# A routed expert kernel: earlier gathers for the first group of a two-group pass, a second group routed in the prologue, own row buffers for each pass

## The chip, the cores and the metric

The kernel runs on one core of a Trainium2 chip. The metric is the device time of one execution in microseconds. A core has five engines with instruction streams of their own: PE (matrix products), DVE (vector work), ACT (activations, copies out of PSUM), POOL (here: indirect transfers) and SP (here: plain transfers). Each runs its stream in order and waits on semaphores.

## What is computed

`x` has 8 units (batch entries) of 512 tokens by 128 channels. Three sublayers follow one another: half a mixture-of-experts layer, a recurrent token mixer, and half the same mixture-of-experts layer again, each on normalised input and added to `x`.

```python
def ffn(x, gate_w, w1, w3, w2):                 # 8 experts, 2 for each token
    probs = softmax(x @ gate_w)
    weights, experts = top_k(probs, 2);  weights /= weights.sum(-1)
    for i in range(8):
        h = silu(x @ w1[i]) * (x @ w3[i])       # 128 -> 512
        out += (h @ w2[i]) * weight_of_expert_i
x = x + 0.5 * ffn(layernorm(x))
x = x + mixer(layernorm(x))                     # k, v, r projections, a scan over 512 tokens, output projection
x = x + 0.5 * ffn(layernorm(x))
```

## The kernel before

**Runs and passes.** The work of the two expert layers is cut into 9 runs (lines 38 to 63). Runs 0 to 3 are the first layer, two units each. Runs 4 to 8 are the second layer, with 2, 2, 2, 1 and 1 units. A pass is a list of rows in memory sorted by expert, each expert's rows padded to tiles of 128. In the first layer each run is a pass of its own; in the second, runs 4 and 5 share a pass, runs 6 and 7 share one, and run 8 has its own. In a shared pass the first run (`OPEN`) computes only its full tiles, and the second (`MORE`) fills up and computes the partly filled ones. There are 177 tiles (steps). Runs begin at tiles 0, 23, 46, 69, 92, 101, 131, 140 and 162; `PEND`, the end of the pass, is 23, 46, 69, 92, 131, 131, 162, 162, 177.

**A tile.** SP loads sorted rows from `rows_in` into `rin`, six loads ahead (line 663; a load holds one or two tiles). PE turns them (line 1228), ACT copies them to `rT` (line 770). PE makes the two up products `pa` and `pb` (line 1237), ACT applies SiLU (line 799), DVE multiplies to `h` (line 1115), PE makes the down product three tiles later (line 1251), ACT copies it and stores it to `rows_out` (lines 780, 786). PE's tile `t` waits for `h` of tile `t-2`.

**Routing.** For each run: norm, split in two 16-bit parts `hi` and `lo`, transposed product with the gate (`turn`, `xnT`, `logits`, `keep`), then choosing (`CHOOSE`, line 90: `pick` to `place2`, `scatter`, `tiles`, `weights`; DVE functions at lines 938 to 1079). POOL then writes the tokens' rows to their slots in `rows_in`: 8 indirect transfers for each unit (`scatter`, line 717). When the tiles of a pass are stored, POOL reads each token's two result rows back: 8 indirect transfers for each unit (`gather`, line 730), and DVE adds them to `x` (`combine`, line 1117). Three gather buffers rotate (`GSLOTS`). After a first-layer combine follows the mixer of that unit, and then the routing of the second-layer run that needs it.

**Zero fills.** Rows that no token takes must be defined, so SP fills `rows_in` from a zero row (lines 614 to 660). There are four memory sets, used by passes 0 to 3 and again by 4 to 6. Sets 0 and 1 are filled, 23 tiles each, by one transfer ahead of the tiles (`FILLED_FIRST`); sets 2 and 3 and the longer tails of sets 0 and 1 in pieces of 256 rows, one per tile from tile 0 (list `later`). A run's first scatter waits until the fills of its set have landed (lines 720 to 725).

**The order.** A planner in the file (`make_plan`, line 218) decides behind which tile each step stands on every engine. It has costs for each step (`WORK`), a model clock for each engine, due times, a few corrections by hand (`DUE_SHIFT`, and `NOT_BEFORE`, earliest tiles for named steps), and it books POOL's transfers by due time, one for each 1.6 us of its own clock (`SPACE`). Steps in `soon(...)` (lines 252 to 265) stand ahead of tile 0 in the order written: the prologue. There run 0 is routed, and run 1 is normalised and its logits kept; run 1's choosing stands among tiles 0 to 9. On POOL a memset (line 755) spaces the transfers.

```python
def send(tile, until):          # line 337: books transfers up to the model time `until`
    ...
        due, asked, name, run, many = first = min(now)          # 344
        free["pool"] = max(free["pool"], asked) + SPACE         # 345
        transfers.append((tile, name, run, *many.pop(0)))       # 346
```

In the order before, run 1's scatters stand at tiles 10 to 18, run 2's at 24 to 27 (nine) and 39 to 41 (seven), run 0's gathers at 28 to 38, run 6's scatters at 120 to 127, run 7's at 134 and 135, run 4's gathers at 136 to 145, run 5's up to 160 with run 8's scatters between, those of runs 6 and 7 from 167. The combines of run 0 stand at tiles 35 and 39, those of run 5 at 163.

Of the kernel before, what the change touches and what calls it, by code (L numbers as in the profile page):

```python
# [21 lines left out]
F32 = mybir.dt.float32  # L22
F16 = mybir.dt.float16
# [4 lines left out]
P = 128  # L28
B, S, D = 8, 512, 128
E, F, TOPK = 8, 512, 2  # L30
FC = F // P
JU = S // P
T = 128
# [4 lines left out]
FIRST = ((2,), (2,), (2,), (2,))  # L38
SECOND = ((2, 2), (2, 1), (1,))
PASSES = FIRST + SECOND  # L40
UNITS = tuple(n for units in PASSES for n in units)
R1 = sum(len(units) for units in FIRST)
RUNS = len(UNITS)
PASS = tuple(i for i, units in enumerate(PASSES) for _ in units)
OPEN = tuple(r + 1 < RUNS and PASS[r + 1] == PASS[r] for r in range(RUNS))
MORE = tuple(r > 0 and OPEN[r - 1] for r in range(RUNS))
SET = tuple(i if i < len(FIRST) else i - len(FIRST) for i in PASS)
SETS = max(SET) + 1
U0 = tuple(sum(UNITS[0 if r < R1 else R1:r]) for r in range(RUNS))
UG = max(UNITS)  # L50
JG = UG * JU
# [5 lines left out]
NQ = tuple(SINGLES + PAIRS[r] if PAIRS[r] else (STEPS[r] + 1) // 2 for r in range(RUNS))  # L57
START = tuple(sum(STEPS[:r]) for r in range(RUNS + 1))
PSTART = tuple(sum(PASS_STEPS[:PASS[r]]) for r in range(RUNS))
PEND = tuple(sum(PASS_STEPS[:PASS[r] + 1]) for r in range(RUNS))  # L60
QSTART = tuple(sum(NQ[:r]) for r in range(RUNS + 1))
ROWS = tuple(max(PASS_STEPS[PASS[r]] for r in range(RUNS) if SET[r] == g) * T for g in range(SETS))
TILES = START[RUNS]
assert all(len(units) <= 2 for units in PASSES) and sum(UNITS[:R1]) == sum(UNITS[R1:]) == B
assert all(OPEN[r] or MORE[r] or STEPS[r] == 2 * PAIRS[r] + SINGLES for r in range(RUNS))
# [12 lines left out]
GSLOTS = 3  # L78
RING = 6
SKEW = 3  # L80
FILLED_FIRST = 2
FILL = 256
PACE = 544
PACES = 4
# [133 lines left out]
def make_plan():  # L218
# [9 lines left out]
    def route(run, normed):  # L228

        chain(CHOOSE, run, 0, (START[run], 0), 0.0, normed)  # L230

    never = 1e9
    route(1, [])
    for run in range(2, R1):
        route(run, [chain(NORM, run, b, (START[run], 1), 0.0) for b in range(UNITS[run])])
    for g in range(R1):
# [6 lines left out]
                route(run, [chain(NORM, run, b, (START[run], 1), 0.0, [mixed[U0[run] + b]])  # L243
                            for b in range(UNITS[run])])
    for run in range(R1, RUNS):
        for b in range(UNITS[run] if PEND[run] < TILES else 0):
            gathered[run, b] = chain(FINISH, run, b, (START[min(run + 2, RUNS - 1)], 3), never)


# [2 lines left out]
    def soon(run, *steps):  # L252
        plan.extend((EARLY, step, run, b) for step, b in steps)
# [6 lines left out]
        soon(0, *[("split", 2)][:b + 1 not in first], ("keep", b))  # L260
        soon(0, *((step, b + 1) for step in ("xnT",) if b + 1 in first))
    soon(0, *((step, 0) for step in CHOOSE))
    soon(1, *(("stats", b) for b in one), ("rsqrt", 0))
    soon(0, *(("split", e) for e in range(3, E)))
    soon(1, *((step, b) for b in one for step in ("norm", "turn", "xnT", "hi", "lo", "logits", "keep")))

    clock, transfers, waiting = Clock(), [], []
    free, held, freed = clock.free, {}, {}
# [58 lines left out]
    def ask(at, due, name, run, units):  # L327

        waiting.append([due, at, name, run, [(b, j, c) for b in units for j in range(JU) for c in range(TOPK)]])

    def in_use(run, unit):

        order = [p[2:] for p in plan if p[1] == "gather"]
        n = order.index((run, unit))
        return n >= GSLOTS and "combine" not in gathered[order[n - GSLOTS]].ends
# [39 lines left out]
    for tile in range(TILES):  # L375
        clock.tile(tile)
        for run in range(RUNS):
            if tile == PEND[run] + SKEW:
                for b in range(UNITS[run]):
                    ask(free["pe"] + LAND, tile + (8 if run < R1 else 60) + 4 * MORE[run] + b, "gather", run, [b])  # L380
                    plan.append((tile, "gather", run, b))
        send(tile, free["pe"])
        begun = free["pe"]
        limits = {"dve": begun + SLIP["dve"], "act": begun + SLIP["act"], "pe": begun + SLIP["pe"]}
        found = choose(limits)
        while found:
            put(found[0], tile, found[1])
            found = choose(limits)
        while any(tile >= START[run] - LEAD and left[run] for run in left) or (
                tile == TILES - 1 and any(c.next() for c in chains)):  # L390
            found, sent = choose(None), len(transfers)
            if found:
                put(found[0], tile, found[1])
            send(tile, 1e8)
            assert found or len(transfers) > sent
    last = [(TILES, step, run, b) for run in range(RUNS) if PEND[run] == TILES
            for step in ("gather", "combine", "write") for b in range(UNITS[run])]
    return plan + last, transfers, clock

# [41 lines left out]
def macaron_kernel(nc, x, channel_vecs, att_w, gate, w1, w3, w2, out):  # L441
    with ExitStack() as ctx:
# [6 lines left out]
        def sem(name):  # L449
            return ctx.enter_context(nc.semaphore(name))  # L450


        rows_in = [nc.dram_tensor(f"rows_in{g}", (ROWS[g], 2 * D), F16, kind="Internal").ap() for g in range(SETS)]
        rows_out = [nc.dram_tensor(f"rows_out{g}", (ROWS[g], D), F32, kind="Internal").ap() for g in range(SETS)]


        xres = sb("xres", [P, B * JU, D])
# [89 lines left out]
        s_stage = [sem(f"stage_in{i}") for i in range(E)]  # L547
        s_w2 = sem("w2_in")
        s_zrow = sem("zrow_made")
        s_fill = [sem(f"rows_zeroed{g}") for g in range(SETS)]  # L550
        s_rest = [sem(f"more_rows_zeroed{g}") for g in range(SETS)]
        s_const = sem("const_made")
        s_uphi = sem("up_hi_made")
        s_uplo = sem("up_lo_made")
# [59 lines left out]
        def pieces(g, start, end, size):  # L614

            return [(g, at, min(at + size, end)) for at in range(start, end, size)]

        fills = [pieces(g, 0, PASS_STEPS[g] * T, ROWS[g] if g < FILLED_FIRST else FILL) for g in range(SETS)]
        rests = [pieces(g, PASS_STEPS[g] * T, ROWS[g], FILL) for g in range(SETS)]


        @block.sync
        def _(sp):
# [7 lines left out]
            def fill(piece, filled):  # L631

                g, start, end = piece
                rows = rows_in[g][start:end, :].rearrange("(r p) c -> p r c", p=P)
                sp.dma_start(rows, zrow[:, None, :].to_broadcast([P, (end - start) // P, 2 * D])).then_inc(filled[g], 16)
# [19 lines left out]
                             w2[e, :, :].rearrange("(c p) d -> p c d", p=P)).then_inc(s_w2, 16)  # L655
            for g in range(2, R1):
                load_x(g)
            for piece in fills[1]:
                fill(piece, s_fill)
            later = [(piece, s_fill) for g in range(2, SETS) for piece in fills[g]]  # L660
            later += [(piece, s_rest) for g in range(SETS) for piece in rests[g]]

            def load(q):
                t = FIRST_STEP[q]
                run, n = run_of(t), TILE_OF[t][2]
                if t == START[run]:
                    sp.wait_ge(s_scat[run], 16 * TOPK * JU * UNITS[run])
                wait(sp, s_turn, q - SLOTS + 1)
                at = (t - PSTART[run]) * T
                sp.dma_start(rin[:, q % SLOTS, 0:n, :],  # L670
                             rows_in[SET[run]][at:at + n * T, :].rearrange("(n p) c -> p n c", p=P)
                             ).then_inc(s_rin[q % SLOTS], 16)

            def step(name, run, b):
# [27 lines left out]
        def _(pool):  # L702
# [12 lines left out]


            def scatter(run, b, j, c):
                g = SET[run]
                at = (U0[run] + b) * JU + j
                if (b, j, c) == (0, 0, 0):  # L720
                    pool.wait_ge(s_slots, run + 1)
                    pool.wait_ge(s_lo, max(count(("lo", "lo_m"), ("lo", run, i)) for i in range(UNITS[run])))
                    pool.wait_ge(s_fill[g], 16 * len(fills[g]))
                    if run >= R1 and rests[g]:
                        pool.wait_ge(s_rest[g], 16 * len(rests[g]))
                pool.indirect_dma_start(  # L726
                    rows_in[g][:], bass.IndirectOffsetOnAxis(ap=slot[:, c, at:at + 1], axis=0),
                    parts[:, at, :], None).then_inc(s_scat[run], 16)

            def gather(run, b, j, c):  # L730
                at = (U0[run] + b) * JU + j
                if (b, j, c) == (0, 0, 0):
                    for k in range(YSLOTS):
                        pool.wait_ge(s_yst[k], 16 * len(range(k, PEND[run], YSLOTS)))
                n = GATHERS.index((run, b))
                if (j, c) == (0, 0) and n >= GSLOTS:
                    pool.wait_ge(s_comb, count(("combine",), ("combine", *GATHERS[n - GSLOTS])))
                pool.indirect_dma_start(  # L738
                    yg[:, n % GSLOTS, c, j, :], None, rows_out[SET[run]][0:PASS_STEPS[PASS[run]] * T, :],
                    bass.IndirectOffsetOnAxis(ap=slot[:, c, at:at + 1], axis=0)).then_inc(  # L740
                        s_last[j] if n + 1 == len(GATHERS) else s_gat[n % GSLOTS], 16)

            def every(run, units):
                return [(run, b, j, c) for b in units for j in range(JU) for c in range(TOPK)]
# [9 lines left out]
                    wait(pool, s_pace, sent - PACES + 1)  # L754
                    pool.memset(pace[:, sent % PACES, :], 0).then_inc(s_pace, 1)  # L755
            for run in range(RUNS):
                for one in every(run, range(UNITS[run] if PEND[run] == TILES else 0)):
                    gather(*one)


# [1 line left out]
        def _(act):  # L762
# [23 lines left out]
            def store(t):  # L786
                run = run_of(t)
                at = (t - PSTART[run]) * T
                act.wait_ge(s_yrow, t + 1)
                act.dma_start(rows_out[SET[run]][at:at + T, :], yrow[:, t % YSLOTS, :]  # L790
                             ).then_inc(s_yst[t % YSLOTS], 16)

            def tile(t):
# [602 lines left out]
```

## Time and profile before

| | |
|---|---|
| median of 3 runs | 611.98 us (611.75 to 612.49) |
| the profiled execution | 611.98 us |
| its span, first to last instruction | 610.1 us |
| PE matrix products | 517.9 us busy, 85% |
| DVE | 423.6 us, 69% |
| ACT | 318.7 us, 52% |
| POOL | 389.0 us, 64% |
| DMA traffic | 59.55 MB, mean 98 GB/s |
| granted TensorE clock, mean | 0.980 |

Busy times overlap, since the engines run side by side. The first 54 us are the prologue, with PE mostly idle; the last 24 us hold the end of PE's work and the last gathers. "Busy" of PE is modelled from pipelined matmuls and is not its peak. A granted clock of 1.00 is 2.4 GHz, 0.50 is 1.2 GHz.

### The profile page before, as it was taken

The numbers are of one execution on the slowest core, as the hardware profiler recorded it, in microseconds if no ns is written. First come the engines' busy times: TensorE is split into PE (matmuls) and PEld (weight loads), VectorE is DVE, ScalarE is ACT, GpSimd is POOL, SyncE is SP. The second block draws the span as 40 slices with busy tenths as digits, with TensorE's granted clock in tenths as the row PEclk, the third lists the DMA queues.
The fourth block names the chain that finished last, engine by engine and source line by source line (L and its number), as shares of the span: only waits on it lengthen the run. The fifth ranks groups of instructions, "written<-read, shape, count | busy, mean of one in ns | idle before, by whom it ended". The sixth has DMA issues, their size and how long they took to land.

```text
span 610.1 us, 18551 instructions
## 1 busy us (share of the span) xinstructions
PE 517.9 (85%) x5866; PEld 474.2 (78%) x5866; DVE 423.6 (69%) x1218; ACT 318.7 (52%) x703; POOL 389.0 (64%) x490
## 2 busy tenths in 40 slices
PE   1234899999999899998999989999999999999930
PEld 1233789898988789877898779898788899998930
DVE  4861963556878998889999895887788766225431
ACT  5432664444584666666585654676465454444410
POOL 1171049499999990399935999102957998955973
PEclk9999999999999999999999999999999999999985
DMA  8963233555232222212321133111121442323332
GB/s 280 328 209 110 69 92 110 145 148 127 83 105 79 67 80 57 71 62 70 83 71 46 58 113 92 45 51 32 53 84 54 122 111 88 102 62 105 85 91 60
DMA packets 89062, 59.55 MB, mean 98 GB/s; under 512 B 10256, under 2 KB 82704, under 8 KB 88976
## 3 DMA queue, kind: packets, MB, share of 16 engines
q1 hardware_dynamic: 55296, 29.97, 16.9%
q0 software_dynamic: 8192, 16.79, 9.0%
q10 hardware_dynamic: 25488, 11.61, 6.7%
q8 instruction: 58, 0.95, 0.7%
q14 instruction: 28, 0.23, 0.1%
HBM read 28.65 MB, written 29.69 MB: 96 GB/s over the span
## 4 chain that ended last, share of the span: by engine, by line
PE 55%; DVE 14%; ACT 12%; POOL 8%; issue 7%; DMA 3%; POOLq 0%; ACTq 0%; DVEq 0%; SPq 0%
PE py L1260 17%; PE pa L1246 14%; PE pb L1246 12%; POOL rows_in L726 3%; ACT xn L818 3%; DVE h L1115 3%; POOL yg L738 3%; PE bkB L1319 2%; PE pT L1233 2%; PE bkB L1298 2%; ACT sil L799 2%; POOL pace L755 2%; PE bkA L1313 2%; DVE stats L905 2%; PE bkA L1298 1%
## 5 line engine op out<-in xcount | busy, mean ns | idle before, releaser
L726 POOL DMA_INDIRECT rows_in<-parts,slot x128 | 134.9, 1054 | 175.7 <-DVE slot L1040 153.8
L1260 PE MATMUL py<-ffn_w,h 128*128 x1416 | 196.2, 282 | 9.4 <-ACT yrow L784 9.0
L1115 DVE TENSOR_TENSOR h<-sil,pb 128x512 f32<-128x512 f32 x177 | 120.7, 686 | 116.8 <-ACT sil L799 76.6
L1260 PEld LDWEIGHTS py<-ffn_w,h 128*128 128x128 f32 x1416 | 172.6, 192 | 15.5 <-issue 12.3
L1246 PE MATMUL pa<-rT,ffn_w 128*128 128x128 f16 (+1 forms) x1752 | 150.3, 232 | 14.9 <-DVE h L1115 11.8
L1246 PE MATMUL pb<-rT,ffn_w 128*128 128x128 f16 (+1 forms) x1752 | 154.4, 232 | 0.0
L738 POOL DMA_INDIRECT yg<-rows_out,slot x128 | 125.1, 978 | 35.0 <-issue 22.8
L1246 PEld LDWEIGHTS pa<-rT,ffn_w 128*128 x1752 | 123.3, 99 | 29.5 <-issue 18.4
L755 POOL MEMSET pace<- 128x544 uint8 x223 | 127.6, 572 | 0.2
L1246 PEld LDWEIGHTS pb<-rT,ffn_w 128*128 x1752 | 121.8, 98 | 6.9
L799 ACT ACTIVATE sil<-pa 128x512 f32<-128x512 f32 x177 | 105.4, 595 | 31.8 <-PE pa L1246 31.7
L784 ACT ACTIVATE yrow<-py 128x128 f32<-128x128 f32 x177 | 48.4, 274 | 85.3 <-PE py L1260 81.1
L779 ACT ACTIVATE rT<-pT 128x512 f16<-128x512 f16 (+1 forms) x112 | 56.8, 507 | 67.6 <-PE pT L1233 63.0
L1233 PE MATMUL pT<-ident,rin 128*128 128x128 f16 x354 | 38.6, 221 | 9.6 <-DMA rin<-rows_in 9.6
L818 ACT ACTIVATE xn<-xres,shift,rstd 128x128 f32<-128x128 f32 x96 | 39.3, 486 | 8.3 <-DVE shift L927 7.0
L1125 DVE SCALAR_TENSOR_TENSOR xres<-yg,wts,xres 128x128 f32<-128x128 f32 x120 | 34.1, 347 | 9.0 <-DMA yg<-rows_out,slot 8.5
L1313 PE MATMUL bkA<-ident,xn 128*128 128x128 f32 x64 | 11.8, 315 | 28.0 <-ACT xn L818 27.2
L1233 PEld LDWEIGHTS pT<-ident,rin 128*128 128x128 f16 x354 | 25.8, 99 | 10.9 <-DMA rin<-rows_in 9.8
L1313 PEld LDWEIGHTS bkA<-ident,xn 128*128 128x128 f32 x64 | 8.5, 165 | 29.3 <-issue 28.1
L935 DVE TENSOR_TENSOR parts<-xn,parts 128x512 f16<-128x512 f32 x24 | 16.4, 688 | 10.5 <-ACT parts L832 10.5
L1298 PE MATMUL bkB<-xT,qkv_w 128*128 128x512 f16 x96 | 23.4, 380 | 0.3 <-ACT xT L848 0.3
L905 DVE BATCH_NORM_STATS2 stats<-xres 128x6 f32<-128x128 f32 x96 | 20.9, 280 | 4.0 <-DMA xres<-in_x 3.5
(156 smaller groups left out, 458.8 us busy)
## 6 DMA issues: line engine op xcount, KB each, us to landing
rows_out<-yrow ACTq DMA_DIRECT2D x177, 64.0 KB, 1.9
rin<-rows_in SPq DMA_DIRECT2D x65, 128.0 KB
rows_in<-zrow SPq DMA_DIRECT2D x34, 128.0 KB, 2.1
shared<-in_w SPq DMA_DIRECT2D x16, 256.0 KB, 6.7
rin<-rows_in SPq DMA_DIRECT2D x47, 64.0 KB
rows_in<-zrow SPq DMA_DIRECT2D x2, 1472.0 KB, 11.2
xres<-in_x SPq DMA_DIRECT2D x4, 512.0 KB, 6.5
ffn_w<-in_w SPq DMA_DIRECT2D x8, 256.0 KB, 4.7
```

The source lines that it names most:

```text
L726: pool.indirect_dma_start(rows_in[g][:], bass.IndirectOffsetOnAxis(ap=slot[:, c, at:at + 1], axis=0), parts[:, at, :], None).then_inc(s_sc ...
L738: pool.indirect_dma_start(yg[:, n % GSLOTS, c, j, :], None, rows_out[SET[run]][0:PASS_STEPS[PASS[run]] * T, :], bass.IndirectOffsetOnAxis( ...
L755: pool.memset(pace[:, sent % PACES, :], 0).then_inc(s_pace, 1)
L779: act.activation(rT[:, q % 2, :, 0:n], pT[:, :, 0:n], ACT.Copy).then_inc(s_rT, 1)
L784: act.activation(yrow[:, t % YSLOTS, :], py[:], ACT.Copy).then_inc(s_yrow, 1)
L799: act.activation(sil[:, t % 2, :], pa[t % 2][:], ACT.Silu, scale=1.0 / WS).then_inc(s_sil, 1)
L818: ins = act.activation(xn[:, at, j, :], xres[:, js, :][:, j, :], ACT.Identity, bias=shift[:, u, j:j + 1], scale=rstd[:, u, j:j + 1])
L1115: dve.tensor_tensor(h[:, t % RING, :], sil[:, t % 2, :], pb[t % 2][:], ALU.mult).then_inc(s_h, 1)
L1233: mm = pe.transpose(pT[:, part, n * T:(n + 1) * T], rin[:, q % SLOTS, n, part * D:(part + 1) * D], ident16[:])
L1246: mm = pe.matmul(bank[:, i * cols:(i + 1) * cols], weight_bytes[:, bass.ds(experts[expert_of(t)] * 4 + at, 2 * P)].bitcast(F16), rT[:, q % ...
L1260: mm = pe.matmul(py[:], h[:, step % RING, at:at + T], w, start=(c == 0), stop=(c == FC - 1))
L1298: mm = pe.matmul(bank[:], qkv_w[:, f, wp, :], xT[:, u % 2, xp, start:start + S], start=(n == 0), stop=(n == 5))
```

## The change

- A gather waits for the end of its own run's rows, `GEND`, in place of the end of the pass, `PEND`. The rows of an opening run all lie in the first 23 tiles of its pass (`HEAD_STEPS`). `GEND` is 23, 46, 69, 92, 115, 131, 154, 162, 177, so it differs for runs 4 (115 for 131) and 6 (154 for 162). The planner asks for gathers three tiles after it.
- Run 1's choosing stands in the prologue, behind the splits 3 to 7, and its scatters are asked for at time 0. In the prologue both its norms now stand ahead of those splits, and its two `lo` steps behind its other steps.
- Each pass has its own `rows_in` and `rows_out`. All of them are filled; the one transfer ahead of the tiles is pass 0's, the others are pieces of 256 rows, one per tile from tile 0: pass 1 at tiles 0 to 11, pass 2 at 12 to 23, pass 3 at 24 to 35, then passes 4 to 6 up to tile 79. A first scatter waits for the pieces of the head of its pass.

`DUE_SHIFT` and `NOT_BEFORE` stay as they are.

```diff
-SET = tuple(i if i < len(FIRST) else i - len(FIRST) for i in PASS)
-SETS = max(SET) + 1
...
-PEND = tuple(sum(PASS_STEPS[:PASS[r] + 1]) for r in range(RUNS))
+HEAD_STEPS = tuple((units[0] * S * TOPK + E * (T - 1)) // T for units in PASSES)
+
+GEND = tuple(PSTART[r] + (HEAD_STEPS if OPEN[r] else PASS_STEPS)[PASS[r]] for r in range(RUNS))
...
-FILLED_FIRST = 2
...
-    route(1, [])
...
-    soon(1, *(("stats", b) for b in one), ("rsqrt", 0))
+    soon(1, *(("stats", b) for b in one), ("rsqrt", 0), *(("norm", b) for b in one))
     soon(0, *(("split", e) for e in range(3, E)))
-    soon(1, *((step, b) for b in one for step in ("norm", "turn", "xnT", "hi", "lo", "logits", "keep")))
+    soon(1, *((step, b) for b in one for step in ("turn", "xnT", "logits", "hi", "keep")), *(("lo", b) for b in one))
+    soon(1, *((step, 0) for step in CHOOSE))
...
+    ask(0.0, START[1] - 3, "scatter", 1, range(UNITS[1]))
...
-            if tile == PEND[run] + SKEW:
+            if tile == GEND[run] + SKEW:
...
-        fills = [pieces(g, 0, PASS_STEPS[g] * T, ROWS[g] if g < FILLED_FIRST else FILL) for g in range(SETS)]
-        rests = [pieces(g, PASS_STEPS[g] * T, ROWS[g], FILL) for g in range(SETS)]
+        fills = [pieces(g, 0, HEAD_STEPS[g] * T, FILL if g else HEAD_STEPS[g] * T) for g in range(len(PASSES))]
+        rests = [pieces(g, HEAD_STEPS[g] * T, PASS_STEPS[g] * T, FILL if g else PASS_STEPS[g] * T)
+                 for g in range(len(PASSES))]
...
-            for piece in fills[1]:
-                fill(piece, s_fill)
-            later = [(piece, s_fill) for g in range(2, SETS) for piece in fills[g]]
-            later += [(piece, s_rest) for g in range(SETS) for piece in rests[g]]
+            for piece in rests[0]:
+                fill(piece, s_rest)
+            later = [(piece, filled) for g in range(1, len(PASSES)) for many, filled in ((fills, s_fill), (rests, s_rest))
+                     for piece in many[g]]
...
                     pool.wait_ge(s_fill[g], 16 * len(fills[g]))
-                    if run >= R1 and rests[g]:
+                    if MORE[run]:
                         pool.wait_ge(s_rest[g], 16 * len(rests[g]))
...
-                        pool.wait_ge(s_yst[k], 16 * len(range(k, PEND[run], YSLOTS)))
+                        pool.wait_ge(s_yst[k], 16 * len(range(k, GEND[run], YSLOTS)))
...
-                    yg[:, n % GSLOTS, c, j, :], None, rows_out[SET[run]][0:PASS_STEPS[PASS[run]] * T, :],
+                    yg[:, n % GSLOTS, c, j, :], None, rows_out[PASS[run]][0:(GEND[run] - PSTART[run]) * T, :],
```

## Rows read from the trace of the kernel before

**Rows 1.** Busy times from 57 to 587 us, sum of six stretches (length, then each engine).
```profile
sum 530.00, PE 502.79 PEld 461.51 DVE 388.62 ACT 294.73 POOL 359.28; mean PE 83.80 PEld 76.92 DVE 64.77 ACT 49.12 POOL 59.88
```
**Rows 2.** DMA issues by line: KB each, median us from issue to landing.
```profile
rows_in<-zrow SPq DMA_DIRECT2D x34, 128.0 KB, 2.1
...
yg<-rows_out,slot POOLq DMA_INDIRECT x128, 2.7
```
**Rows 3.** Timeline of ACT, prologue: start us, us, engine, line, operation, [idle before].
```profile
22.45 4.83 ACT L768 ACTIVATE ffn_w<-shared 128x1024 f16<-128x1024 f32 x5
32.83 1.65 ACT L818 ACTIVATE xn<-xres,shift,rstd 128x128 f32<-128x128 f32 x4 [5.55 <-DVE shift L927]
...
44.00 0.20 ACT L840 ACTIVATE logit<-bkB 128x32 f32<-128x32 f32 x1 [1.51 <-PE bkB L1319]
...
54.12 0.84 ACT L772 ACTIVATE qkv_w<-yg 128x768 f16<-128x768 f32 x1
...
56.27 0.60 ACT L799 ACTIVATE sil<-pa 128x512 f32<-128x512 f32 x1
```
**Rows 4.** Timeline of DVE, prologue.
```profile
19.17 0.22 DVE L950 TENSOR_REDUCE mx<-logit 128x8 f32<-128x64 f32 x1
...
27.80 0.16 DVE L1079 TENSOR_SCALAR wts<-ed 128x8 f32<-128x8 f32 x1
...
43.20 0.16 DVE L1091 TENSOR_SCALAR omix<-vecs 128x3 f32<-128x3 f32 x1
...
44.60 0.27 DVE L1096 TENSOR_SCALAR yg<-att_raw,omix 128x128 f32<-128x128 f32 x1
```
**Rows 5.** Timeline of PE, tiles 2 and 5.
```profile
60.07 0.89 PE L1246 MATMUL pa<-rT,ffn_w 128*128 128x256 f16 x6
...
68.04 0.81 PE L1246 MATMUL pa<-rT,ffn_w 128*128 128x256 f16 x6 [1.80 <-DVE h L1115]
```
**Rows 6.** Timeline of SP's queue, tiles 11, 17, 23 (and 24).
```profile
86.54 0.33 SPq L635 DMA_DIRECT2D rows_in<-zrow  x1
...
112.71 0.36 SPq L670 DMA_DIRECT2D rin<-rows_in  x1
...
121.59 2.31 SPq L635 DMA_DIRECT2D rows_in<-zrow  x2
```
**Rows 7.** Timeline of POOL: first and last (16th) scatter of run 1, first of run 2.
```profile
83.35 1.15 POOL L726 DMA_INDIRECT rows_in<-parts,slot  x1 [33.86 <-DVE slot L1040]
...
109.38 0.96 POOL L726 DMA_INDIRECT rows_in<-parts,slot  x1 [0.16 <-issue]
...
118.66 0.96 POOL L726 DMA_INDIRECT rows_in<-parts,slot  x1 [7.75 <-DVE slot L1040]
```
**Rows 8.** Timeline of PE, tile 22: run 1's first rows are turned.
```profile
118.51 0.39 PE L1233 MATMUL pT<-ident,rin 128*128 128x128 f16 x4
```
**Rows 9.** Timeline of DVE: the two combines of run 0.
```profile
152.82 2.31 DVE L1125 SCALAR_TENSOR_TENSOR xres<-yg,wts,xres 128x128 f32<-128x128 f32 x8
...
163.35 2.31 DVE L1125 SCALAR_TENSOR_TENSOR xres<-yg,wts,xres 128x128 f32<-128x128 f32 x8
```
**Rows 10.** Timeline of POOL: last scatter of run 6, first of run 7.
```profile
450.54 0.97 POOL L726 DMA_INDIRECT rows_in<-parts,slot  x1 [0.16 <-issue]
...
459.65 0.96 POOL L726 DMA_INDIRECT rows_in<-parts,slot  x1 [7.41 <-DVE slot L1040]
```
**Rows 11.** Timeline of SP's queue: run 7's first two loads.
```profile
475.06 0.90 SPq L670 DMA_DIRECT2D rin<-rows_in  x2
```
**Rows 12.** Timeline of PE, tile 139: run 7's first rows are turned.
```profile
482.62 0.39 PE L1233 MATMUL pT<-ident,rin 128*128 128x128 f16 x4
```
**Rows 13.** Stretch of 10 us: busy times, granted clock, DMA share, GB/s.
```profile
360.00:370.00 10.00, 7.95 (x85) 7.57 (x83) 7.83 (x12) 3.82 (x8) 9.18 (x12) 0.83 0.39 111
```
**Rows 14.** Timeline of POOL: first of the last eight gathers.
```profile
591.00 0.94 POOL L738 DMA_INDIRECT yg<-rows_out,slot  x1 [0.30 <-issue]
```
**Rows 15.** Timeline of ACT's queue: the last store.
```profile
586.88 0.33 ACTq L790 DMA_DIRECT2D rows_out<-yrow  x1
```

More of the change, by code:

```diff
@@ L59 @@
 PSTART = tuple(sum(PASS_STEPS[:PASS[r]]) for r in range(RUNS))
-PEND = tuple(sum(PASS_STEPS[:PASS[r] + 1]) for r in range(RUNS))
+HEAD_STEPS = tuple((units[0] * S * TOPK + E * (T - 1)) // T for units in PASSES)
+GEND = tuple(PSTART[r] + (HEAD_STEPS if OPEN[r] else PASS_STEPS)[PASS[r]] for r in range(RUNS))
 QSTART = tuple(sum(NQ[:r]) for r in range(RUNS + 1))
-ROWS = tuple(max(PASS_STEPS[PASS[r]] for r in range(RUNS) if SET[r] == g) * T for g in range(SETS))
 TILES = START[RUNS]
@@ L245, in make_plan @@
     for run in range(R1, RUNS):
-        for b in range(UNITS[run] if PEND[run] < TILES else 0):
+        for b in range(UNITS[run] if GEND[run] < TILES else 0):
             gathered[run, b] = chain(FINISH, run, b, (START[min(run + 2, RUNS - 1)], 3), never)
@@ L395, in make_plan @@
             assert found or len(transfers) > sent
-    last = [(TILES, step, run, b) for run in range(RUNS) if PEND[run] == TILES
+    last = [(TILES, step, run, b) for run in range(RUNS) if GEND[run] == TILES
             for step in ("gather", "combine", "write") for b in range(UNITS[run])]
@@ L450, in sem @@
             return ctx.enter_context(nc.semaphore(name))
-        rows_in = [nc.dram_tensor(f"rows_in{g}", (ROWS[g], 2 * D), F16, kind="Internal").ap() for g in range(SETS)]
-        rows_out = [nc.dram_tensor(f"rows_out{g}", (ROWS[g], D), F32, kind="Internal").ap() for g in range(SETS)]
+        rows_in = [nc.dram_tensor(f"rows_in{g}", (PASS_STEPS[g] * T, 2 * D), F16, kind="Internal").ap() for g in range(len(PASSES))]
+        rows_out = [nc.dram_tensor(f"rows_out{g}", (PASS_STEPS[g] * T, D), F32, kind="Internal").ap() for g in range(len(PASSES))]
         xres = sb("xres", [P, B * JU, D])
@@ L549, in macaron_kernel @@
         s_zrow = sem("zrow_made")
-        s_fill = [sem(f"rows_zeroed{g}") for g in range(SETS)]
-        s_rest = [sem(f"more_rows_zeroed{g}") for g in range(SETS)]
+        s_fill = [sem(f"rows_zeroed{g}") for g in range(len(PASSES))]
+        s_rest = [sem(f"more_rows_zeroed{g}") for g in range(len(PASSES))]
         s_const = sem("const_made")
@@ L670, in load @@
                 sp.dma_start(rin[:, q % SLOTS, 0:n, :],
-                             rows_in[SET[run]][at:at + n * T, :].rearrange("(n p) c -> p n c", p=P)
+                             rows_in[PASS[run]][at:at + n * T, :].rearrange("(n p) c -> p n c", p=P)
                              ).then_inc(s_rin[q % SLOTS], 16)
@@ L717, in scatter @@
             def scatter(run, b, j, c):
-                g = SET[run]
+                g = PASS[run]
                 at = (U0[run] + b) * JU + j
@@ L756, in _ @@
             for run in range(RUNS):
-                for one in every(run, range(UNITS[run] if PEND[run] == TILES else 0)):
+                for one in every(run, range(UNITS[run] if GEND[run] == TILES else 0)):
                     gather(*one)
@@ L789, in store @@
                 act.wait_ge(s_yrow, t + 1)
-                act.dma_start(rows_out[SET[run]][at:at + T, :], yrow[:, t % YSLOTS, :]
+                act.dma_start(rows_out[PASS[run]][at:at + T, :], yrow[:, t % YSLOTS, :]
                              ).then_inc(s_yst[t % YSLOTS], 16)
```

## The prediction

> **What bounds the kernel now.** I read the busy times of the stretch of tiles first. From tile 0 to the last down product PE works 502.8 of 530 us [rows 1], so it is the bound there and 27 us are all that could be won in the tiles; a wait put in front of PE is lost. Ahead of tile 0 stand 54 us of prologue, behind it a tail. Next I read the five queues one by one. In the tiles POOL sends one transfer per 1.7 us (fifteen steps in 26.0 us [rows 7]: transfer, memset, issue), and it is strictly in order: whatever stands ahead of a transfer delays it. SP is in order as well: its zero fills stand one per tile in the loop, behind a wait for a y copy some three tiles back. In the tail PE has ended, the last store is issued at 586.9 [rows 15], and POOL begins the last unit's eight gathers at 591.0 [rows 14], because it is still busy with those of runs 6 and 7. The end comes 19.1 us behind that start (span 610.1).
>
> **The change part by part.** The profiled execution took 611.98 us, which is also the median of the runs; the sum is made against that.
>
> *1. Run 1 is routed in the prologue.* Routing a group takes DVE from 19.2 to 28.0, 8.7 us [rows 4]. Between the end of `weights` (44.9) and tile 0 DVE has nothing to do, so most of it is covered. But the order ahead of it changes too: both norms of run 1 now precede the splits 3 to 7 on ACT, where before the splits ran first, from 22.5 for 4.8 us, while ACT would otherwise wait for rstd until 32.8 [rows 3]. Now they follow the norms. Run 1's last logits were copied at 44.0; with 4.8 us of splits in the chain that is 48.8, less some 1.2 for the transposes that PE makes meanwhile: 47.6. Then DVE: choosing 8.7, `weights` 1.7 (43.2 to 44.9 [rows 4]): 58.0. ACT's qkv copy waits for that, and from its start to the first SiLU are 2.15 us (54.12 to 56.27 [rows 3]): SiLU at 60.2, product at 60.9. PE starts tile 2 at 61.6 instead of 60.07 [rows 5]. The DVE chain behind it (tile 1's product, the qkv split, tile 2's product, then run 2's statistics, for which PE already waits 1.8 us at 68.04 [rows 5]) is late by the same. **+1.5**, bounds 0 (cover holds) and +3.5.
>
> *2. The same work is gone from tiles 0 to 9:* 8.7 us of DVE. At PE's mean idle share, 27 of 530 us [rows 1], the 63 us from tile 0 to tile 22 hold 3.2 us, and part of that is ACT's. **-1.0**, bounds -3.2 and 0.
>
> *3. Run 1's scatters.* Their slots are ready by 56, yet `scatter` waits for all of `fills[1]`. Those 2944 rows were one transfer ahead of the tiles; now they are 12 pieces issued at tiles 0 to 11. The piece of tile 11 goes out at 86.54 in this trace [rows 6] and a piece lands 2.1 us later [rows 2]: first scatter at 88.7 instead of 83.35 [rows 7], 5.4 late. Nothing else stands behind it on POOL until run 2. But SP's load of run 1's first rows, at 112.7 [rows 6], becomes 118.1 and lands (no row has a load's landing; a piece of equal size takes 2.1) at 120.2, while PE wants them at 118.5 [rows 8], 1.7 of waiting; some of it may fall together with PE's wait for routing run 2. **+1.5**, bounds 0 and +2.5.
>
> The Trainium skill (DMA: Bandwidth & Descriptors, Rules for kernel authors) says to issue a DMA early and wait for its semaphore late. The change does the reverse with this fill; by that rule an early fill would hide and part 3 would cost nothing. The rows show the pace of the tiles in it instead.
>
> *4. Run 2's scatters and run 0's gathers.* SP stands at tile 17 in the load just named, so fills 17 to 23 wait behind it; run 2 needs the one of tile 23. Before, it went out 8.9 us after the load (121.59 [rows 6]); now at 127.0 if the whole distance stays, at 123.1 if SP catches up with PE. Landed: 125.2 to 129.1; I take 127.5. Run 2's first scatter was at 118.66 [rows 7], so POOL is 8.8 late, 7.3 against tiles that are 1.5 late. Behind nine of these scatters stand run 0's sixteen gathers: the eighth starts near 145.7 and lands at 148.4 (2.7 [rows 2]), the sixteenth near 159.3, landing 162.0. Their combines stand at 152.8 and 163.4 on DVE [rows 9]: slacks 4.4 and 1.4. DVE stalls 2.9 and then 3.0 more. At the first PE has next to no slack; at the second it has heavy products of its own ahead. **+4.0**, bounds +2 and +6. Clock after it: **+0.5**.
>
> *5. Gathers of runs 4 and 6 from tile 118 and 157, instead of 134 and 165.* The planner books one POOL transfer per 1.6 us of its own time. Run 6's sixteen scatters stand at tiles 120 to 127 in its order; run 7's are held back by `"scatter7.0": 133`. Before, nothing was asked in between, and on the chip run 7's first scatter went right when its slots came, 459.65 [rows 10]. Now run 4's gathers are asked at 118, and at two per tile some 13 of them are booked between. POOL is free of run 6 at 452.2 [rows 10]; 13 x 1.7 later it is 474.3, so run 7 starts 14.6 late. SP's load of its first rows at 475.06 [rows 11] becomes 489.7, landed 491.8; PE wants them at 482.6 [rows 12], in tile 139. **+9.0**, bounds +4 (10 gathers ahead) and +11. SP waits in that load, but its other loads are for run 7 too. DVE's earlier combine (2.3 us) lies inside the stall.
>
> *6. The clock after that stall.* In the stretch from 360 to 370, with PE busy 7.95 of 10 us, the granted clock was 0.83 [rows 13]: it fell to 1.2 GHz for a while, which is 1.7 us of PE. **+1.5**, bounds 0 and +3. The Trainium skill (TensorE: Matmul & The Clock Gate, Part 1) also has the idle array at 1.2 GHz, and says not to fit a ramp; by it I would put 0 here.
>
> *7. The tail.* With eight gathers of run 6 sent earlier POOL is free when the last store lands, near 586.88 + 2 [rows 15]; start at 588.9 instead of 591.0: **-2.1**. `"combine5.0": 163` stays, so the two combines at tile 163 still block DVE, and run 6's second unit still waits for their slot. A combine more among the last tiles: **+0.5**.
>
> *8. At nothing:* own rows for each pass mean 44 more fills of 128 KB at tiles 36 to 79, one per tile, a stretch in which SP otherwise issues only loads, six tiles ahead of their use, and in which no scatter is ready so early; if that cover fails, each delays a load by up to 2.1 us [rows 2]. Gather ranges are only shorter.
>
> Sum: +1.5 - 1.0 + 1.5 + 4.0 + 0.5 + 9.0 + 1.5 - 2.1 + 0.5 = +15.4: **627 us**.
>
> **Rivals.** *Run 7 is not displaced* (gathers booked behind its scatters): parts 5 and 6 go, +4.9, 617. For: run 6's scatters are late enough in the plan that a small shift decides; against: fifteen tiles lie between ask and hold. 16%. *The fills do not bite* (PE early enough to pull them, DVE free): parts 1 to 4 give 0, +8.9, 621. 14%. *Faster:* neither bites because the prologue absorbs both and only the DVE relief and the tail count: -1.0 - 2.1 + 0.5, 609.4. It decides the matter when run 7's first load goes out by 480.5 (5.4 us of slack) and the first combine finds its rows. 10%. *Nothing moves:* gains and small waits cancel within 1.2 us. 7%.
>
> **Numbers.** The forecast, both waits, 53%, own range 620 to 633. A measurement here tells 0.2%, 1.2 us. Faster 0.10, same 0.07, slower 0.83. Range 613 to 633: it takes in the forecast and the two one-sided cases (83%, less what lies beyond the bounds).
>
> **What would show it.** Right: run 1's first scatter starts just after the fill of tile 11; POOL is idle before run 2's first scatter with a fill as the releaser; DVE waits for yg before the first two combines; gathers stand between run 6's and run 7's scatters; PE waits 7 to 10 us for rin in tile 139 and runs slow behind it; the last gathers start 2 us after the last store. Wrong: no idle PE ahead of tile 139, or the first combine without a wait. If the time is under 613, part 5 has failed.

## The result, and the profile after

The changed kernel takes 628.54 us (median of 4, 627.42 to 630.67) where the kernel before takes 612.00: 1.027 times as long, 95% interval 1.0242 to 1.0304. The profiled execution took 627.73 us with a span of 625.9; the span before was 610.1, so the rows below have to explain 15.8 us.

The page of the changed kernel first: PE's busy time, then its busy share and its granted clock in 40 equal slices of the span:

```profile
PE 521.3 (83%) x5866; PEld 476.8 (76%) x5866; DVE 426.2 (68%) x1218; ACT 319.1 (51%) x703; POOL 394.7 (63%) x499
...
PE   1234899999699899998999989998999599999940
...
PEclk9999999999799999999999999999999899999995
```

The same two lines of slices before:

```profile
PE   1234899999999899998999989999999999999930
...
PEclk9999999999999999999999999999999999999985
```

PE does the same 5866 instructions. Two slices stand out, the 11th (156 to 172 us) and the 32nd (485 to 501 us), each in part idle and at a lower clock. The waits of PE, by what it waited for (us in total, times, longest us), show what it waited for there, after and then before:

```profile
PE pa L1247 <- DVE h L1116: 19.1, 14, 5.7
PE pT L1234 <- DMA rin<-rows_in: 11.0, 4, 7.5
```

```profile
PE pa L1246 <- DVE h L1115: 11.8, 12, 2.0
PE pT L1233 <- DMA rin<-rows_in: 9.6, 2, 9.0
```

The 9.0 us before are a wait ahead of tile 0.

The useful measure is the start of the product (h) of each tile on DVE's timeline, after against before. This table gives the difference in us, worked out from such starts:

```
tile             0    1    12    20    23    30    36    40    44   100   102   131   134   139   146   170   176   span
after - before  3.1  1.0  -0.5  -0.4   0.7  -0.4   5.7   8.0   6.9   7.4   5.9   6.6   8.7  14.2  17.0  17.0  17.9  15.8
```

**The first loss, tile 36.** POOL's timeline, with the last number in brackets the idle time before: run 1's first scatter, run 2's first scatter, run 0's first gather.

```profile
88.44 0.96 POOL L727 DMA_INDIRECT rows_in<-parts,slot  x1 [38.22 <-DMA rows_in<-zrow]
...
128.21 0.96 POOL L727 DMA_INDIRECT rows_in<-parts,slot  x1 [12.66 <-DMA rows_in<-zrow]
...
143.52 0.98 POOL L739 DMA_INDIRECT yg<-rows_out,slot  x1 [0.16 <-issue]
```

Both first scatters now wait for a zero fill; against [rows 7] they are 5.1 and 9.6 us later. SP's queue shows the link between them: it stood in run 1's load from 101 us, with run 2's last fills behind it.

```profile
100.82 0.36 SPq L636 DMA_DIRECT2D rows_in<-zrow  x1
116.29 0.36 SPq L671 DMA_DIRECT2D rin<-rows_in  x1
116.69 0.47 SPq L636 DMA_DIRECT2D rows_in<-zrow  x1
...
124.08 1.73 SPq L636 DMA_DIRECT2D rows_in<-zrow  x2
```

The eighth gather of run 0 completes the rows of its first unit. DVE waits for them, and PE for DVE:

```profile
155.31 0.95 POOL L739 DMA_INDIRECT yg<-rows_out,slot  x1 [0.16 <-issue]
```

```profile
158.46 2.31 DVE L1126 SCALAR_TENSOR_TENSOR xres<-yg,wts,xres 128x128 f32<-128x128 f32 x8 [5.92 <-DMA yg<-rows_out,slot]
...
171.33 2.32 DVE L1126 SCALAR_TENSOR_TENSOR xres<-yg,wts,xres 128x128 f32<-128x128 f32 x8 [1.05 <-DMA yg<-rows_out,slot]
```

```profile
163.06 1.46 PE L1247 MATMUL pa<-rT,ffn_w 128*128 128x128 f16 x12 [5.69 <-DVE h L1116]
```

**The second loss, tile 139.** POOL after run 6's scatters: first and last of 13 gathers of run 4, then run 7's first scatter, 21.7 us later than in [rows 10].

```profile
458.86 0.98 POOL L739 DMA_INDIRECT yg<-rows_out,slot  x1 [0.17 <-issue]
...
479.61 0.95 POOL L739 DMA_INDIRECT yg<-rows_out,slot  x1 [0.16 <-issue]
481.30 1.01 POOL L727 DMA_INDIRECT rows_in<-parts,slot  x1 [0.17 <-issue]
```

PE turns run 7's first rows only after this wait; in [rows 12] there was none:

```profile
498.26 0.61 PE L1234 MATMUL pT<-ident,rin 128*128 128x128 f16 x4 [7.45 <-DMA rin<-rows_in]
```

**The clock behind each.** Stretches of 2 us; the columns are window, length, busy time (instructions) of PE, PEld, DVE, ACT and POOL, granted clock, DMA share, GB/s.

```profile
162.00:164.00 2.00, 0.94 (x10) 0.94 (x11) 1.86 (x7) 0.00 (x0) 1.77 (x3) 0.50 0.25 66
164.00:166.00 2.00, 2.00 (x20) 2.00 (x19) 1.76 (x9) 1.23 (x4) 1.83 (x3) 0.50 0.20 54
166.00:168.00 2.00, 2.00 (x15) 1.94 (x15) 0.78 (x3) 1.93 (x6) 1.84 (x3) 0.56 0.31 85
...
498.00:500.00 2.00, 1.74 (x17) 1.74 (x17) 0.00 (x0) 1.09 (x3) 1.69 (x3) 0.50 0.93 234
500.00:502.00 2.00, 1.97 (x10) 1.67 (x8) 0.69 (x1) 1.97 (x5) 1.83 (x3) 0.50 1.02 304
502.00:504.00 2.00, 1.97 (x25) 1.77 (x25) 0.69 (x1) 0.94 (x3) 1.83 (x3) 0.93 0.35 91
```

After each idle time PE works at 0.50 (1.2 GHz) for 4 to 5 us. As an estimate, busy time times the missing clock gives 0.94 x 0.50 + 2.00 x 0.50 + 2.00 x 0.44 = 2.4 us behind the first and 2.0 us behind the second.

**The two ends.** In the prologue the first product comes at 60.53 and PE starts tile 2 at 61.46 ([rows 5]: 60.07). In the tail POOL has been idle for 11.5 us when its last eight gathers start. The profile names no releaser; in the code they wait for the stores, and the last store was issued at 604.10, 2.6 us ahead (4.1 us before, [rows 14] and [rows 15]):

```profile
604.10 0.33 ACTq L791 DMA_DIRECT2D rows_out<-yrow  x1
```

```profile
606.73 0.95 POOL L739 DMA_INDIRECT yg<-rows_out,slot  x1 [11.52 <-issue]
```

### The profile page after: what moved, and what is told of

It is laid out like the page before. It is cut to its first block, busy times and chain, and to the rows that moved or that the text cites. A ratio compares the mean times of both kernels' runs of the same rounds, so it can differ in the third digit from the quotient of the medians.

```text
span 625.9 us, 18574 instructions
## 1 busy us (share of the span) xinstructions
PE 521.3 (83%) x5866; PEld 476.8 (76%) x5866; DVE 426.2 (68%) x1218; ACT 319.1 (51%) x703; POOL 394.7 (63%) x499
## 4 chain that ended last, share of the span: by engine, by line
PE 38%; POOL 24%; DVE 13%; ACT 11%; issue 7%; DMA 5%; POOLq 0%; ACTq 0%; DVEq 0%; SPq 0%
PE py L1261 12%; PE pa L1247 9%; POOL rows_in L727 9%; POOL pace L756 8%; PE pb L1247 8%; POOL yg L739 6%; ACT xn L819 3%; DVE h L1116 2%; PE bkB L1320 2%; ACT sil L800 2%; PE bkB L1299 2%; PE pT L1234 2%; DVE xres L1126 1%; DMA yg<-rows_out,slot 1%; DVE stats L906 1%
## 5 line engine op out<-in xcount | busy, mean ns | idle before, releaser
L756 POOL MEMSET pace<- 128x544 uint8 x232 | 133.0, 573 | 0.2
L1320 PEld LDWEIGHTS bkB<-gate_w,xnT 128*128 128x128 f32 x128 | 18.8, 226 | 8.3 <-issue 7.2
L1320 PE MATMUL bkB<-gate_w,xnT 128*128 128x8 f32 x128 | 18.9, 275 | 7.3 <-ACT xnT L837 7.3
```

The lines of the kernel that those rows point to most:

```text
L1320: mm = pe.matmul(bkB[:, j * E:(j + 1) * E], xnT[:, j * P:(j + 1) * P], gate_w[:], start=True, stop=True)
```

## The experiments

My theory had two independent causes: the fill of run 1's rows in pieces, and run 4's gathers booked ahead of run 7's scatters. Of the first four runs one undoes the first cause, one the second, one both, and one makes the prologue's change alone. "Before" in each result is the kernel before, timed beside it.

**e1, the fill whole again** (in the changed kernel; `fills` and `later` in `sync`, lines shortened to what changes):

```
-  fills: FILL if g else HEAD_STEPS[g] * T
+  fills: FILL if g > 1 else HEAD_STEPS[g] * T
+  for piece in fills[1]:
+      fill(piece, s_fill)
-  later: for g in range(1, len(PASSES))
+  later: for g in range(2, len(PASSES))
```

> The changed kernel with the fill of run 1's rows as one transfer ahead of the tiles again; all else as in the change. Fill theory (the 12 pieces at tiles 0 to 11 make run 1's scatters late, SP then stands in run 1's load with run 2's fills behind it, POOL is late for run 0's gathers, DVE waits for yg and PE for DVE): the loss of 7 us between tile 35 and tile 44 goes, about 621.5 us; run 1's first scatter near 60, run 2's first scatter near 119, DVE's first two combines without a wait of over 2 us. Rival (the loss comes from the new prologue, which starts the tiles 3 us late and orders DVE's steps otherwise): 628 to 629 us as before the edit, tile 36 still 5 to 6 us late. Second rival (the two losses are one and the same slack: PE late at tile 36 gives POOL time at tile 139, so that without the first the second grows): 626 or more, tile 139 later against tile 138 by over 10 us.

Measured: 623.42 us (621.02 to 627.2) beside 612.03, ratio 1.0149 to 1.0243. The product of tile 40 is 0.2 us late against before, not 8.0. The second loss stays what it was: 1.7 us late at tile 131, 12.2 at tile 146. Both rivals fall. The runs scatter more than I expected, and the median is 2 us over my number. The edit also puts run 2's pieces back to tiles 0 to 11; e9 below takes the two fills apart.

**e2, run 4's gathers late in the plan:**

```
-  if tile == GEND[run] + SKEW:
+  if tile == (sum(PASS_STEPS[:PASS[run] + 1]) if run == 4 else GEND[run]) + SKEW:
```

> The changed kernel, but the planner asks for run 4's gathers only at the tile at which it did before the change (end of the pass); the fills stay in pieces. Theory (13 gathers ahead of run 7's scatters make its rows late): no gather between run 6's and run 7's scatters, PE's wait of 7.45 us at tile 139 and the half clock behind it go, about 618.5 us. Rival (tile 139 is late because run 7's slots are late: run 3's mixing, DVE's order or the combine moved forward): 628 us, the wait at tile 139 stays over 5 us.

Measured: 618.38 us beside 612.03, ratio 1.0085 to 1.0119. POOL's idle time ahead of run 7's scatters is as long as in [rows 10], and its cause is the slots:

```profile
467.54 0.96 POOL L727 DMA_INDIRECT rows_in<-parts,slot  x1 [7.40 <-DVE slot L1041]
```

PE turns run 7's rows without a wait; tile 131 and tile 146 are both 7.9 us late. So nothing of the second loss is left, the 2.1 us that the table has between tiles 131 and 134 among it.

**e3, both edits:**

> Both edits together. Theory: both losses go and are independent, so that only the new prologue, the relief of DVE in tiles 0 to 9 and the earlier gathers of run 6 in the tail are left: 611 us, between 609.5 and 612.5. Rival (the prologue costs 3 us that nothing gives back): 614 to 615. Rival (44 more fills cost PE time): a loss spread over tiles 36 to 79, over 613.

Measured: 611.47 us beside 612.03, ratio 0.9980 to 0.9999. The losses are nearly additive: by the spans (625.9 changed, 621.0, 617.0, 610.8) the fill costs 6.2 us where it stands alone, the gathers 10.2, and together 15.1. From tile 44 to tile 100 the shift stays at 1.8 us. With run 1's fill whole there are 68 small fills where the kernel before has 36 and the change 80, so 32 of the 44 more are in it, at tiles 36 to 67, and they cost nothing.

**e6, run 1 routed in the prologue and nothing else** (on the kernel before):

```
-    route(1, [])
-    soon(1, *(("stats", b) for b in one), ("rsqrt", 0))
+    soon(1, *(("stats", b) for b in one), ("rsqrt", 0), *(("norm", b) for b in one))
...
+    soon(1, *((step, 0) for step in CHOOSE))
...
+    ask(0.0, START[1] - 3, "scatter", 1, range(UNITS[1]))
```

> The kernel before with nothing but run 1 routed in the prologue (fill of run 1 whole, memory shared, gathers as before). Theory: tile 0 is 3 us late, the tiles give 2 to 3 us back by tile 20, run 1's scatters start near 60: 612 us, between 611 and 613. Rival (the prologue makes the loss at tile 36): 617 us or more. Rival (first tiles give nothing back): 615.

Measured: 612.46 us beside 612.03, ratio 0.9996 to 1.0019: no difference. Tile 0 is 3.8 us late, tile 12 only 0.5, and it stays there. Part 1 and part 2 of the prediction cancel.

**e4, the pieces alone** (on the kernel before):

```
-FILLED_FIRST = 2
+FILLED_FIRST = 1
-            for piece in fills[1]:
-                fill(piece, s_fill)
-            later = [(piece, s_fill) for g in range(2, SETS) for piece in fills[g]]
+            later = [(piece, s_fill) for g in range(1, SETS) for piece in fills[g]]
```

> The kernel before with nothing but the fill of run 1's rows cut into 12 pieces at tiles 0 to 11 (so run 2's pieces move to tiles 12 to 23 as in the change); run 1 is still routed in the tiles, memory shared. Fill theory: the pieces alone make the loss between tile 35 and tile 44; run 1's first scatter at 88 to 89, run 2's first at 126 to 128, about 618.5 us (616 to 620). Rival (the pieces only bite together with the late start of the tiles from the prologue): 612 to 614.

**e5, the early gathers alone** (on the kernel before: `GEND` as in the change, in the planner, in POOL's waits and in the gather ranges):

> The kernel before with nothing but the first groups' gathers allowed and planned from the end of their own steps. Theory: 13 gathers go ahead of run 7's scatters, PE waits in tile 139 and runs slow behind it: a loss of 10 to 12 us there; without the first loss POOL is not late, so the wait may be up to 1 us less than in the first edit of the change. With 2 us back in the tail: 620.5 us (619 to 623). Rival (what costs at tile 139 in the change needs the other parts): 612 or less, 610 if only the tail counts.

Measured for these two: 631.77 and 627.24 us, but the kernel before took 626.06 us beside them (624.31 to 629.33). These runs were on a chip where it is 14 us slower. The places are still plain: in e4 the shift grows from 0.7 us at tile 35 to 8.3 at tile 40, and POOL's two first scatters stand at 88.88 and 128.36; in e5 PE waits 7.31 us for run 7's rows. So pieces alone make the first loss, without the new prologue, and gathers alone the second. The totals can't be read against 612, and e4's was not taken again on another chip, so its forecast of 618.5 stays untested. In e4 PE, ACT and DVE all stop near the last tiles, with no cause in the trace:

```profile
599.64 0.28 ACT L782 ACTIVATE yrow<-py 128x128 f32<-128x128 f32 x1 [8.05 <-remote]
...
600.15 2.05 PE L1258 MATMUL py<-ffn_w,h 128*128 x8 [8.68 <-issue]
```

**e7, splits first**, e3 with one line more moved:

```
-    soon(1, *(("stats", b) for b in one), ("rsqrt", 0), *(("norm", b) for b in one))
+    soon(1, *(("stats", b) for b in one), ("rsqrt", 0))
     soon(0, *(("split", e) for e in range(3, E)))
+    soon(1, *(("norm", b) for b in one))
```

> Both edits of before together (whole fill, run 4's gathers late in the plan) and the prologue's splits 3 to 7 ahead of run 1's norms on ACT again, as before the change; run 1 is still routed in the prologue. Theory of part 1: what delays the first product by 3 us is that the splits stand behind the norms, so tile 0 comes back to 57.4 to 58, the first twenty tiles gain 0.5 to 2 us through the work that DVE no longer has there: 610.3 us (609 to 611.3). Rival (DVE's longer chain itself is the delay, the order does nothing): tile 0 at 60 to 61 and 611.5 us. Rival (the gain of the first tiles is taken back by the next wait for a fixed time, the gathers of run 0): tile 0 early, 611.5 us all the same.

**e8, e7 with run 6's first statistics held** (`NOT_BEFORE`: `"stats6.0": 102`):

> The kernel of the run above with run 6's first statistics (1.3 us of DVE) held back from tile 99 to tile 102. PE waits 1.9 us for DVE at tile 101 there and the clock falls behind it in four of the six kernels with a profile so far. Theory: wait and fall go, 2.0 to 2.7 us less than the run above, 608 us. Rival (the wait returns at the next product, since DVE has the same work): no difference.

Measured on the same slow chip: 614.58 and 614.53 us beside 626.06. Between themselves e7 and e8 don't differ. The wait at tile 101 is still there, as the rival had it:

```profile
364.59 1.04 PE L1250 MATMUL pa<-rT,ffn_w 128*128 128x128 f16 x12 [1.90 <-DVE h L1119]
```

The next three runs repeat e5 and e7, with a profile of the kernel before beside them.

> The kernel before, unchanged, with a profile of its own on this chip. In the last four runs the kernel before took 626.1 us where it had taken 612.0, and in the profile of the kernel with the pieces alone PE waited 8.7 us for its own instructions (issue) at 591 to 600, ACT and DVE also without a cause in the profile, while POOL sent unpaced gathers every 1.25 us. If that stall belongs to the tail of before (16 gathers of runs 6 and 7 left for after the planned ones, beside the last tiles): where this kernel takes 624 or more again, its profile has PE idle by 7 us or more between 575 and 590; where it takes 612, it has not.

> The kernel before with the early gathers alone, a second time. Where the kernel before takes 612: 620.5 us (619 to 623), the wait of 7.3 us for rin at tile 139 is there and 2 us come back in the tail. Where the kernel before takes 624 or more: again about 627, because the early gathers of run 6 leave no unpaced gathers beside the last tiles and so have no stall there. Rival (the stall has nothing to do with the gathers): 634 or more on such a chip.

> Whole fill, run 4's gathers late in the plan, splits first in the prologue: a second time. Where the kernel before takes 612: 610.3 us (609 to 611.3); where it takes 624 or more: 614.5 us again. Rival (the order in the prologue is worth nothing): 611.5 us beside 612.

Measured, on a chip where the kernel before takes 611.93: the kernel before 611.91 again, e5 622.25 (ratio 1.0136 to 1.0182), e7 610.23 (0.9959 to 0.9979). e5's rows have the whole second loss, again with 13 gathers ahead of run 7; here is the wait:

```profile
494.09 0.61 PE L1235 MATMUL pT<-ident,rin 128*128 128x128 f16 x4 [7.53 <-DMA rin<-rows_in]
```

e7 is the fastest kernel of the study, 0.3% ahead of the kernel before and 18 us of the changed one. Its profile is 0.8 us ahead at tile 100 and 2.3 at tile 102: the 1.5 us between are the clock behind one wait (last section), so not all of the lead is the order's. Its splits on ACT stand ahead of the norms again, and the first product comes at 58.31, not 60.53:

```profile
22.75 4.82 ACT L772 ACTIVATE ffn_w<-shared 128x1024 f16<-128x1024 f32 x5
33.13 3.19 ACT L822 ACTIVATE xn<-xres,shift,rstd 128x128 f32<-128x128 f32 x8 [5.56 <-DVE shift L931]
```

The stall near the last tiles was in none of the profiles of this chip, so the question of `before_again` stays open on its other side: whether the kernel before has it on the slow chip was not seen. That e5 and e7 lost 5.0 and 4.4 us there and the kernel before 14 fits it, no more.

**e9, run 1's fill in pieces, run 2's whole** (on e7, lines shortened):

```
-  fills: FILL if g > 1 else HEAD_STEPS[g] * T
+  fills: FILL if g not in (0, 2) else HEAD_STEPS[g] * T
-  for piece in fills[1]:
+  for piece in fills[2]:
-  later: for g in range(2, len(PASSES))
+  later: for g in range(1, len(PASSES)) if g != 2
```

> The kernel of the last run but with the roles of the two fills changed: run 1's rows in 12 pieces at tiles 0 to 11, as in the change, and run 2's rows as one transfer ahead of the tiles. Theory (the pieces of run 1 cost little by themselves; the loss at tile 36 comes because they push run 2's pieces behind SP's blocked load of run 1): run 1's first scatter near 88.5, its first load late, PE waits up to 1 us for it at tile 22, but run 2's first scatter starts when POOL is asked, near 119, and there is no wait of 6 us for yg: 610.2 to 611.5 us where the kernel before takes 612. Rival (late scatters of run 1 alone are the loss): 616 us or more.

Measured: 611.92 us beside 612.43 (ratio 0.9983 to 1.0003), 0.4 over the range and far from the rival's 616. POOL and PE:

```profile
87.81 0.96 POOL L730 DMA_INDIRECT rows_in<-parts,slot  x1 [37.74 <-DMA rows_in<-zrow]
117.78 0.97 POOL L730 DMA_INDIRECT rows_in<-parts,slot  x1 [2.79 <-DVE slot L1044]
```

```profile
118.60 0.40 PE L1237 MATMUL pT<-ident,rin 128*128 128x128 f16 x4 [1.01 <-DMA rin<-rows_in]
121.84 0.82 PE L1250 MATMUL pa<-rT,ffn_w 128*128 128x256 f16 x6 [1.05 <-DVE h L1119]
```

Run 1's scatters start within 0.6 us of their time in the change, yet tile 36 shows no loss: it is 0.9 us late like tile 23. The pieces of run 1 cost 2.1 us by themselves (tile 20 to tile 23: -1.1 to +1.0), twice what I had allowed here. The large loss needs run 2's pieces behind them.

## Why the prediction was right, step by step

It said 627, range 613 to 633, both waits likeliest; 628.5 came, with both. The places and chains were right. That the sum came so close (+15.4 against 15.8 by the spans) is partly luck: 1.7 us too little in part 4 met 1.5 us at tile 101 that are no work of the change.

*Part 1, +1.5.* Right: choosing and weights end at 57.7 (58.0 predicted), product at 60.53 (60.9), tile 2 at 61.46 (61.6). e7 shows the cause, the splits behind the norms: with them ahead the product comes at 58.31. *Part 2, -1.0:* the tiles got back 1.7 us between tiles 3 and 12. Together -0.5 at tile 12 where I had +0.5; e6 confirms that they cancel.

*Part 3, +1.5:* +1.1 (tile 20 to 23), but the next wait gave it back at tile 30: PE waited 1.47 us there before and 0.38 after. The rule of the Trainium skill that was weighed (DMA: Bandwidth & Descriptors, Rules for kernel authors: issue early, wait late) holds for this fill: with it issued ahead of the tiles (e1) run 1's first scatter starts at 55.27 and waits for its slots alone.

*Part 4, +4.0 and +0.5 of clock.* The place, the chain and the releasers were right, the size was not. I put POOL 8.8 us late and the tiles 1.5 late, so 7.3 against each other; it was 9.6 and the tiles 0.3 early, 9.9. Take off the slack of 4.4 and DVE's first wait is 5.5; it was 5.92. The second fell to 1.05, because the first had moved the tiles. PE lost nearly all of it in one piece (5.69), and the clock took 2.4 us more, not 0.5. From tile 23 to tile 44 that is +6.2, the 1.1 given back at tile 30 and 1.1 after tile 40 taken off, where I had 4.5. The step that failed is "7.3 against tiles that are 1.5 late": tiles that are early against a transfer that stands at a fixed time only wait longer.

*Parts 5 and 6, +9.0 and +1.5.* 13 gathers, as counted; run 7's first scatter 15.1 us late against the tiles (14.6 predicted). From tile 131 to tile 146 the loss is 10.4, predicted 10.5, but split otherwise. The wait is 7.45. Another 2.1 come two tiles before: run 4's combine, moved forward, stands on a DVE that has no room there. I had put it "inside the stall". Where it costs, it shortens the wait behind it.

```profile
471.89 2.31 DVE L1126 SCALAR_TENSOR_TENSOR xres<-yg,wts,xres 128x128 f32<-128x128 f32 x8
```

e2, with neither that combine nor run 4's gathers there, has no such step; e5_again, with both, has it (2.3 us late at tile 131, 4.4 at 134). The two were not taken apart.

*The clock, both places.* I put 1.5 us for part 6 from [rows 13], where PE had waited about 2 us, and 0.5 for part 4 from no row; behind waits of 5.7 and 7.5 us it cost 4.4. The Trainium skill (TensorE: Matmul & The Clock Gate, Part 1) puts the ramp under 1% of a typical span for modelling, and would leave it out. 4.4 of 625.9 us is 0.7%, so the figure agrees, and yet it is over a quarter of what the change costs.

*Part 7, -2.1 and +0.5:* net -1.2 (17.0 late at tile 170, 15.8 at the end) where I had -1.6. The gathers start 1.5 us sooner behind the last store, not 2.1, because they start 2.6 us behind its issue, where I had 2. The extra combine stands on DVE right ahead of the last product and makes it 0.9 late, but the last store is only 17.2 late, so 0.2 is what it costs:

```profile
596.32 2.31 DVE L1126 SCALAR_TENSOR_TENSOR xres<-yg,wts,xres 128x128 f32<-128x128 f32 x8 [0.33 <-DMA yg<-rows_out,slot]
598.67 0.69 DVE L1116 TENSOR_TENSOR h<-sil,pb 128x512 f32<-128x512 f32 x1
```

*Part 8, nothing:* right for the 32 fills that e3 has; in the changed kernel the shift grows by 0.5 us from tile 44 to tile 100.

*Not in the sum:* 1.5 us come back at tile 101, told below. The table's steps add up: -0.5 to tile 12, +0.1 to tile 20, +1.1 to 23, +6.2 to 44, +0.5 to 100, -1.5 to 102, +0.7 to 131, +10.4 to 146, +0.9 to 176 and -2.1 to the end, 15.8; predicted 15.4.

## What to carry to other kernels

When the order of the tiles sends a queue into a wait, everything behind it in that queue is late too: before moving a fill into a loop, look at which loads stand between its pieces, and for whom the last piece is. When a dependence is loosened, check who is asked earlier than who in a planner; a transfer that nobody waits for was put ahead of one that PE waits for, and keeping the looser wait but the old order took all of that loss away. Time won ahead of a transfer at a fixed time buys nothing but a longer wait.

## What the runs showed that I had not expected

**The same wait, two clocks.** At tile 101 every kernel has PE waiting 1.9 to 2.05 us for DVE. In the 3 us behind it the granted clock was 0.54 to 0.78 in nine of fourteen profiles and 1.00 in five. Before, and after:

```profile
362.80:365.80 3.00, 3.00 (x29) 2.88 (x30) 2.93 (x5) 0.60 (x1) 2.83 (x3) 0.70 0.22 59
```

```profile
370.00:373.00 3.00, 3.00 (x36) 2.81 (x37) 2.93 (x5) 0.60 (x1) 2.83 (x3) 1.00 0.24 57
```

e7 fell there on one chip (0.54) and not on the other (1.00), with 1.91 and 1.92 us of waiting. Four of the five profiles at 1.00, the changed kernel's among them, have 1.5 us less from tile 100 to tile 102 than the kernel before, the fifth (e8) 1.2. So the 1.5 us that the changed kernel wins at tile 101 are this and no work of the change; what decides it stays open.

**One chip, 14 us slower for one kernel and 4.4 for another.** The kernel before took 626.1 us there, e5 627.2 and e7 614.6. Part of it is in the rows: waits of PE for its own instructions near 210, 289, 306 and 510 us in e7, 0.98 to 1.44 us each, of which its profile on the other chip has none, and in e4 the one of 8.68 us.

```profile
510.45 1.05 PE L1250 MATMUL pa<-rT,ffn_w 128*128 128x128 f16 x12 [1.44 <-issue]
```

The long one fell while POOL sent gathers every 1.25 us without the memset between them, beside the last tiles; e5, e7 and e8, which have no such gathers there, have no such stall. The kernel before sends 16 such gathers there too, from 579.75 us on, and has no such stall at 612 us, nor has e6. So the gathers alone don't make it; whether they do on the slow chip was not tried.
